# Experts of a decoder block on one core: w1 and w3 held by TensorE, tokens passed through

## The chip, the cores and the metric

The kernel runs on 1 core of one Trainium2 chip. The metric is the device time of the whole kernel in microseconds. TensorE's clock has two levels here, 1.2 and 2.4 GHz; the profile gives the granted clock of a stretch as a share of the higher one.

## The reference, cut to what matters

A decoder block with layer norm behind each part runs on x of 32 sequences x 128 tokens x 128 features, f32: first a state space layer, then cross attention, then a mixture of 8 experts. Each token goes to its best two experts, and an expert is

```
h   = silu(x @ w1[e].T) * (x @ w3[e].T)        # 128 -> 512, twice
out = out + wte[:, e] * (h @ w2[e].T)          # 512 -> 128
```

The product with w2 sums over the 512 values of h. A TensorE product sums over partitions, so both of its operands must have h's 512 values on partitions (in 4 chunks of 128).

## The kernel before, in words

**Stages.** The state space layer and the attention take the first 840 us: 8 groups of 4 sequences, in an order written out by hand for each engine. Every token's row is scattered to two places in DRAM (`xg`), one area per expert. Then a table is built on VectorE: for each of NT = 72 tiles of 128 rows, its expert and its first row. The expert stage goes over the 72 tiles, and the last stage adds the two results of each token and normalises.

**The expert stage.** Each engine has its own loop over tiles, and semaphores order them. In the words of the code, with b the parity of the tile:

- SyncE, `rows_in` (L387 to L389): reads the tile's first row from the table and starts the load of 128 rows to `xs` (named qk in the profile), 4 buffers.
- TensorE, `rows_t` (L1677): transposes the rows to bank 7. `up` (L1679 to L1683): `value_load` reads the expert from the table (L1680), then two products of 512 columns, with the tokens `xsT` as the held operand and w1 or w3 passing, to bank b (named pair_a; w1) and bank 2+b (pair_b; w3). `gated_t` (L1688): 4 transposes of the gated rows, to bank 4+b (y_ps). `down` (L1691 to L1696): another `value_load`, then 4 products with w2 (named prob), summed in bank 6.
- ScalarE: `x_out` (L829) copies the transposed rows to `xsT` (qk), `silu` (L833) turns bank b into `sl` (zabs), and the copy at L846 brings the transposed gated rows to `gT` (decays).
- VectorE: `gate` (L1191) multiplies `sl` by bank 2+b into `gg` (zpos). The copy at L1232 empties bank 6 into `ys` (aoT). `destinations` (L1196 to L1200) are three operations on 128x1 for a later tile's scatter. In the first 8 tiles `gate_gaps` adds up to one operation a tile.
- GpSimd (L566) scatters `ys` to `y2` in DRAM, 4 buffers.

**The order.** In turn j, TensorE issues rows_t(j+3), up(j+2), gated_t(j+1), down(j). VectorE issues gate(j+2), the copy of y(j), destinations(j+3). down(j) waits at L1694 and L1695: for gT of tile j, and until j copies at L1232 are done (`y_sb` starts at 1), that is those of tiles 0 to j-1. gate(j) waits until both products of up(j) are done (`up_ps`) and for silu(j). After the loop SyncE waits for the last scatters, and loads the results with `results_in` (L407); three of the four buffers of these loads are parts of `u` and `sres`.

Of the kernel before, what the change touches and what calls it, by code (L numbers as in the profile page):

```python
# [9 lines left out]
ACT = mybir.ActivationFunctionType  # L10
AX = mybir.AxisListType

P = 128
# [6 lines left out]
E, F = 8, 512  # L20
FC = F // P
STRIDE = B * L + P
NT = (2 * B * L + E * (P - 1)) // P + 1
# [21 lines left out]
def build(nc, a, out):  # L45
    ctx = ExitStack()
    with ctx:
        def sb(name, shape, dt=F32):
            return ctx.enter_context(nc.sbuf_tensor(name, shape, dt))

        def sem(name):
            return ctx.enter_context(nc.semaphore(name))

        ident = sb("ident", [P, P])
# [36 lines left out]
        w1 = sb("w1", [P, E, F])  # L91
        w3 = sb("w3", [P, E, F])
# [12 lines left out]
        u = sb("u", [P, 2, 2, T])  # L105
# [8 lines left out]
        decays = sb("decays", [P, 2, 2 * T])  # L114
# [27 lines left out]
        w2 = prob[:, :, :, :, :].rearrange("p a j c m -> p (a j) c m")  # L142
# [45 lines left out]
        table = sb("table", [P, 2, NT + 8], I32)  # L188
# [3 lines left out]
        xsT = free[:, 4 * ROW:4 * ROW + 2 * P].rearrange("p (b n) -> p b n", b=2)  # L192
        sl = zabs
        gg = zpos
        gT = decays[:, 0, :].rearrange("p (b c n) -> p b c n", b=2, c=FC)
        ys = aoT[:, 0:4 * D].rearrange("p (b d) -> p b d", b=4)
        spare = sb("spare", [P, 8])
        place = sb("place", [P, 8])
# [12 lines left out]
        bank = [x[:, i] for x in (pair_a, pair_b, y_ps) for i in range(2)]  # L211
# [13 lines left out]
        pad_sb mask_sb s_ps s_neg p_sb rden_sb rden_wide_sb pT_ps pT_sb pTd_sb pv_ps rdenT_ps rdenT_sb rdenTd_sb aoT_sb wo_ps  # L225
        ln2_stat ln2_var ln2_log ln2_rstd x2_sb x2T_ps x2T_sb lg_ps lg_sb route rank_ps pos_sb row_sb scat
        tail tail_store table_sb table_link gap_sb gexp_sb gate_link
        xs_load0 xs_load1 xs_load2 xs_load3 xsT_ps xsT_sb up_ps silu_sb gate_sb gT_ps gT_sb y_ps_s y_sb place_sb dest_sb y_out0 y_out1 y_out2 y_out3
        yk_load0 yk_load1 yk_load2 yk_load3 yk_sb acc_ps f_stat f_var f_log f_rstd fin_sb fin_store0 fin_store1""".split()
        s = {n: sem(n) for n in names}  # L230

# [66 lines left out]
        def parts(m):  # L298

            return (m - 1 if m else None), (m + 1 if m + 1 < G else None), (m + 2 if m + 2 < G else None)  # L300
# [5 lines left out]
        def _(sp):  # L306
# [90 lines left out]
            with sp.Fori(0, NT // 4) as it:  # L397
                for b in range(4):
                    j = it * 4 + b
# [6 lines left out]
            def results_in(g, b):  # L406
                sp.dma_start(yk[b].rearrange("p (s k) d -> p s (k d)", k=2), y2r[g]).then_inc(s[f"yk_load{b}"], 16)  # L407
# [4 lines left out]

            for b in range(4):
                sp.wait_ge(s[f"y_out{b}"], NT // 4 * 16)
            for b in range(4):
                results_in(b, b)
            for g in range(G):
# [153 lines left out]
        def _(act):  # L571
            A = nc.scalar.activation
# [175 lines left out]
            for m in range(G):  # L748
                w, e, c = parts(m)
# [77 lines left out]
            def x_out(j, b):  # L827
                act.wait_ge(s["xsT_ps"], 1 + j + 1)
                A(xsT[:, b, :], bank[7][:, b * P:(b + 1) * P], ACT.Copy).then_inc(s["xsT_sb"], 1)  # L829

            def silu(j, b):
                act.wait_ge(s["up_ps"], 1 + 2 * j + 1)
                A(sl[:, b, :], bank[b], ACT.Silu).then_inc(s["silu_sb"], 1)  # L833

            nc.scalar.preload_act_table_set("silu_and_others")
            x_out(0, 0)
            x_out(1, 1)
            silu(0, 0)
            act.wait_ge(s["up_ps"], 1 + 2)
            x_out(2, 0)  # L840
            silu(1, 1)
            with act.Fori(0, NT // 2) as it:
                for b in range(2):
                    j = it * 2 + b
                    act.wait_ge(s["gT_ps"], j + 1)
                    A(gT[:, b], bank[4 + b].rearrange("p (c n) -> p c n", c=FC), ACT.Copy).then_inc(s["gT_sb"], 1)  # L846
                    x_out(j + 3, 1 - b)
                    silu(j + 2, b)
            nc.scalar.preload_act_table_set("natural_log_exp_and_others")
            act.wait_ge(s["gap_sb"], 1)  # L850
            A(gexp, gap, ACT.Exp, scale=-1.0).then_inc(s["gexp_sb"], 1)
# [25 lines left out]
        def _(dve):  # L877
            v_ = nc.vector
# [12 lines left out]
            for h in range(2):  # L891
                last = v_.tensor_scalar(d_diag[:, h, :], ident[:, :], d_col[:, h:h + 1], None, ALU.mult)
# [182 lines left out]
            for m in range(G):  # L1075
                w, e, c = parts(m)
# [111 lines left out]
            def gate(j, b):  # L1188
                dve.wait_ge(s["up_ps"], 1 + 2 * j + 2)
                dve.wait_ge(s["silu_sb"], j + 1)  # L1190
                TT(gg[:, b, :], sl[:, b, :], bank[2 + b], ALU.mult).then_inc(s["gate_sb"], 1)  # L1191

            def destinations(j, load, turn, slot):
                dve.wait_ge(s[f"xs_load{load}"], turn * 16 + 16)
                second = xs[:, load, D + 1:D + 2]
                v_.tensor_scalar(spare[:, slot:slot + 1], second, 0.0, j128[:, bass.ds(j, 1)], ALU.is_lt, ALU.mult)  # L1196
                v_.scalar_tensor_tensor(place[:, slot:slot + 1], second, t_e[:, bass.ds(j, 1)], xs[:, load, D:D + 1],
                                        ALU.is_equal, ALU.add).then_inc(s["place_sb"], 1)
                dve.wait_ge(s["place_sb"], j + 1)
                TT(dest[:, slot:slot + 1], spare[:, slot:slot + 1], place[:, slot:slot + 1], ALU.add).then_inc(s["dest_sb"], 1)  # L1200
# [24 lines left out]
            def eight_tiles(it):  # L1225
                for b in range(8):
                    j = it * 8 + b
                    gate(j + 2, b % 2)
                    dve.wait_ge(s["y_ps_s"], j + 1)
                    if not (isinstance(it, int) and b < 4):  # L1230
                        dve.wait_ge(s[f"y_out{b % 4}"], (2 * it + b // 4) * 16)
                    v_.tensor_copy(ys[:, b % 4, :], bank[6][:, b % 2 * P:(b % 2 + 1) * P]).then_inc(s["y_sb"], 1)  # L1232
                    destinations(j + 3, (b + 3) % 4, 2 * it + (b + 3) // 4, (b + 3) % 8)
                    if isinstance(it, int):
                        gate_gaps(b)

            for j in range(3):
                destinations(j, j, 0, j)
            gate(0, 0)
            gate(1, 1)  # L1240
            eight_tiles(0)
            with dve.Fori(1, NT // 8) as it:
                eight_tiles(it)
# [36 lines left out]
        def _(pe):  # L1280
            MM = nc.tensor.matmul
            TR = nc.tensor.transpose
# [301 lines left out]
            for m in range(G):  # L1584
                w, e, c = parts(m)
# [88 lines left out]
            def rows_t(j, b, turn, load):  # L1674
                pe.wait_ge(s[f"xs_load{load}"], turn * 16 + 16)
                pe.wait_ge(s["xsT_sb"], j)
                TR(bank[7][:, b * P:(b + 1) * P], xs[:, load, 0:D], ident[:, :]).then_inc(s["xsT_ps"], 1)  # L1677

            def up(j, b):  # L1679
                e = pe.value_load(table[0:1, 0, bass.ds(j, 1)], min_val=0, max_val=E - 1)  # L1680
                pe.wait_ge(s["xsT_sb"], j + 1)
                MM(bank[b], xsT[:, b, :], w1[:, bass.ds(e, 1), :].rearrange("p a f -> p (a f)"), start=True, stop=True).then_inc(s["up_ps"], 1)  # L1682
                MM(bank[2 + b], xsT[:, b, :], w3[:, bass.ds(e, 1), :].rearrange("p a f -> p (a f)"), start=True, stop=True).then_inc(s["up_ps"], 1)  # L1683

            def gated_t(j, b):
                pe.wait_ge(s["gate_sb"], 1 + j + 1)
                for c in range(FC):
                    last = TR(bank[4 + b][:, c * P:(c + 1) * P], gg[:, b, c * P:(c + 1) * P], ident[:, :])  # L1688
                last.then_inc(s["gT_ps"], 1)

            def down(j, b):  # L1691
                e = pe.value_load(table[0:1, 0, bass.ds(j, 1)], min_val=0, max_val=E - 1)
                pe.wait_ge(s["gT_sb"], j + 1)
                pe.wait_ge(s["y_sb"], 1 + j)  # L1694
                for c in range(FC):  # L1695
                    last = MM(bank[6][:, b * P:(b + 1) * P], gT[:, b, c, :], w2[:, bass.ds(e, 1), c, :].rearrange("p a d -> p (a d)"),  # L1696
                              start=(c == 0), stop=(c == FC - 1))
                last.then_inc(s["y_ps_s"], 1)

            pe.wait_ge(s["table_sb"], 1)  # L1700
            pe.wait_ge(s["w13_load"], 32)
            pe.wait_ge(s["w2_load"], 16)
            rows_t(0, 0, 0, 0)
            rows_t(1, 1, 0, 1)
            up(0, 0)
            rows_t(2, 0, 0, 2)
            up(1, 1)
            gated_t(0, 0)
            with pe.Fori(0, NT // 4) as it:
                for b in range(4):  # L1710
                    j = it * 4 + b
                    rows_t(j + 3, 1 - b % 2, it + (b + 3) // 4, (b + 3) % 4)
                    up(j + 2, b % 2)
                    gated_t(j + 1, 1 - b % 2)
                    down(j, b % 2)

            def sums(g):
                at(pe, "fin_sb", S * (g - 3))
# [51 lines left out]
```

## Time and profile before

| | |
|---|---|
| median of 3 runs | 1138.08 us (1131.46 to 1140.45) |
| profiled execution | 1135.38 us |
| its span | 1133.5 us, granted clock 0.951 on average |
| TensorE busy | 962.6 us, 85% of the span |
| VectorE busy | 697.1 us, 62% |
| ScalarE busy | 720.5 us, 64% |
| GpSimd busy | 576.0 us, 51% |

The span runs from the first to the last instruction, and 1.9 us lie around it. Busy shares are means over stages that have different limits. The expert stage runs from about 857 to 1093 us.

### The profile page before, as it was taken

The page shows a single profiled execution, that of the slowest core. Times are in us where ns is not written, and L with a number is a line of the kernel's source. Part 1 is how long each engine was busy: PE and PEld are TensorE (multiplying, and loading weights), DVE is VectorE, ACT ScalarE, POOL GpSimd, SP SyncE. Part 2 cuts the span into 40 slices and gives each one's busy share as a digit, 9 for nine tenths or more (in the row PEclk, how much of TensorE's full clock was granted, in tenths as well). Part 3 has the DMA queues.
Part 4 walks back from the last instruction along what each step waited for, and adds up shares of the span by engine and source line. Part 5 has one row for each costly group of instructions (what it writes and reads, how often), then busy time and mean ns, then how long its engine had stood idle before and what let it go on. Part 6 is the DMA issues. An engine that isn't in the chain of part 4 may idle for free.

```text
span 1133.5 us, 28078 instructions
## 1 busy us (share of the span) xinstructions
PE 962.6 (85%) x9703; PEld 543.2 (48%) x9704; DVE 697.1 (62%) x1371; ACT 720.5 (64%) x2212; POOL 576.0 (51%) x395
## 2 busy tenths in 40 slices
PE   6799889989788888979888885976937999999997
PEld 2344544444354445435444542543434666666662
DVE  0467667786577767657766794796653544444437
ACT  3567966876696677669667882964822444444446
POOL 2578258457726954782696388268041333333320
PEclk9889999999899999989999996998977999999999
DMA  4606104201500520050042005003131111111134
GB/s 113 138 15 132 30 1 96 66 2 38 133 12 4 124 54 3 17 136 28 4 107 60 4 16 137 2 4 118 50 119 44 41 41 42 42 42 42 42 105 151
DMA packets 69227, 66.69 MB, mean 59 GB/s; under 512 B 9728, under 2 KB 63104, under 8 KB 68736
## 3 DMA queue, kind: packets, MB, share of 16 engines
q1 hardware_dynamic: 63856, 55.59, 19.8%
q0 software_dynamic: 4352, 8.99, 2.4%
q8 instruction: 69, 1.13, 0.4%
q10 hardware_dynamic: 912, 0.67, 0.2%
q14 instruction: 38, 0.31, 0.1%
HBM read 49.09 MB, written 16.13 MB: 58 GB/s over the span
## 4 chain that ended last, share of the span: by engine, by line
PE 45%; POOL 21%; issue 20%; ACT 8%; DVE 5%; DMA 1%; SPq 0%; POOLq 0%; DVEq 0%; ACTq 0%
POOL hst L494 8%; PE pair_a L1682 6%; PE pair_b L1683 6%; PE bank L1696 6%; POOL prob L494 6%; ACT prob L692 5%; POOL xg L526 4%; PE y_ps L1404 3%; PE y_ps L1688 3%; PE pair_b L1484 3%; PE bank L1302 2%; PE y_ps L1484 2%; PE bank L1495 2%; PE pair_a L1518 2%; PE pair_a L1382 1%
## 5 line engine op out<-in xcount | busy, mean ns | idle before, releaser
L651 ACT ACTIVATE decays<-w,a_neg 128x256 f32<-128x256 f32 x512 | 220.5, 509 | 30.2 <-DVE hst L920 17.6
L494 POOL TENSOR_TENSOR hst<-hst,c_rep 128x1024 f32<-128x1024 f32 x64 | 151.4, 2372 | 73.8 <-DVE hst L920 73.1
L494 POOL TENSOR_TENSOR prob<-prob,c_rep 128x1024 f32<-128x1024 f32 x56 | 133.2, 2381 | 57.3 <-DVE prob L920 56.7
L566 POOL DMA_INDIRECT y<-aoT,dest x72 | 69.6, 966 | 173.2 <-DVE aoT L1232 168.8
L920 DVE TENSOR_TENSOR_SCAN prob<-decays,pair_b 128x1024 f32<-128x1024 f32 x32 | 73.1, 2284 | 69.4 <-issue 54.6
L692 ACT ACTIVATE prob<-pair_b,nmax 128x128 f32<-128x128 f32 x256 | 90.4, 399 | 22.4 <-DVE nmax L974 22.3
L1191 DVE TENSOR_TENSOR zpos<-zabs,pair_b 128x512 f32<-128x512 f32 x74 | 50.8, 687 | 81.3 <-PE pair_b L1683 80.2
L1404 PE MATMUL y_ps<-hst,sum 128*32 128x256 f32 x512 | 74.4, 442 | 24.4 <-POOL prob L494 24.4
L692 ACT ACTIVATE prob<-y_ps,nmax 128x128 f32<-128x128 f32 x256 | 90.8, 415 | 0.0
L526 POOL DMA_INDIRECT xg<-x_all,pos x64 | 64.8, 1013 | 35.8 <-DVE pos L1066 23.7
L920 DVE TENSOR_TENSOR_SCAN prob<-decays,pair_a 128x1024 f32<-128x1024 f32 x32 | 73.0, 2281 | 13.5 <-ACT decays L651 9.9
L1682 PE MATMUL pair_a<-w,qk 128*128 x148 | 77.7, 607 | 0.5 <-ACT qk L829 0.5
L1683 PE MATMUL pair_b<-w,qk 128*128 x148 | 76.5, 599 | 0.0
L1696 PE MATMUL bank<-prob,decays 128*128 x576 | 76.1, 275 | 0.0
L1495 PE MATMUL bank<-ident,prob 128*128 128x128 f32 x512 | 70.7, 279 | 5.3 <-ACT pT L702 5.3
L846 ACT ACTIVATE decays<-y_ps 128x512 f32<-128x512 f32 x72 | 43.0, 598 | 50.2 <-PE y_ps L1688 49.5
L1404 PE MATMUL y_ps<-prob,sum 128*32 128x256 f32 x512 | 74.5, 442 | 0.0
L1382 PE MATMUL pair_b<-w,du_tok 64*32 64x256 f32 x2048 | 72.1, 390 | 2.4 <-DVE prob L920 2.3
L486 POOL TENSOR_TENSOR w<-diag,b_tok 128x1024 f32<-128x1024 f32 x32 | 60.6, 1925 | 26.3 <-ACT b_tok L633 26.3
L920 DVE TENSOR_TENSOR_SCAN hst<-decays,pair_b 128x1024 f32<-128x1024 f32 x32 | 72.6, 2270 | 1.6 <-PE pair_b L1382 1.6
L833 ACT ACTIVATE zabs<-pair_a 128x512 f32<-128x512 f32 x74 | 44.2, 597 | 45.4 <-PE pair_a L1682 45.4
L1302 PE MATMUL bank<-xT,w_conv 128*128 128x512 f32 x112 | 62.1, 676 | 10.1 <-ACT xT L581 10.1
(281 smaller groups left out, 2186.0 us busy)
## 6 DMA issues: line engine op xcount, KB each, us to landing
w<-d_dram SPq DMA_DIRECT2D x64, 256.0 KB
c_rep<-c_dram SPq DMA_DIRECT2D x64, 128.0 KB, 3.4
qk<-xg SPq DMA_DIRECT2D x79, 65.0 KB, 1.9
d_dram<-zpos SPq DMA_DIRECT2D x8, 512.0 KB, 3.0
xn<-in_x SPq DMA_DIRECT2D x8, 256.0 KB, 3.0
cn<-in_ctx SPq DMA_DIRECT2D x8, 256.0 KB, 3.3
mask_b<-in_mask SPq DMA_DIRECT2D x8, 256.0 KB, 3.4
w<-in_w1T SPq DMA_DIRECT2D x1, 2048.0 KB, 8.4
```

The lines of the kernel that those rows point to most:

```text
L494: g_.tensor_tensor(by_state(ring(k)), by_state(ring(k)), c_rep[:, :, toks[r]].rearrange("p q (i t) -> p i q t", i=2), ALU.mult).then_inc(s ...
L526: pool.indirect_dma_start(xg[:, :], bass.IndirectOffsetOnAxis(ap=pos[:, t, k:k + 1], axis=0), x2_all[:, w * S + t, :], None).then_inc(s["s ...
L651: last = A(by_state(decays[:, k % 2, :])[:, :, q, :], delta_rep[:, b, toks[r]].rearrange("p (i t) -> p i t", i=2), ACT.Exp, scale=a_neg[:, ...
L692: last = A(prob[:, t % 2, c, j, :], bank[2 + c][:, j * L:(j + 1) * L], ACT.Exp, bias=nmax[:, t % 2, h:h + 1], accum_out=den[:, t % 2, h:h ...
L920: v_.tensor_tensor_scan(ring(k), decays[:, k % 2, :], pair(k)[:, :, :].rearrange("p i c -> p (i c)"), 0.0, ALU.mult, ALU.add).then_inc(s[" ...
L1302: last = MM(bank[b].rearrange("p (s t) -> p s t", s=S), w_conv[:, k, h * P:(h + 1) * P], xT[:, :, k:k + L], start=(k == 0), stop=(k == KCO ...
L1382: last = MM(pair(k)[32 * j:32 * j + 32, i, :].rearrange("p (q y t) -> p q y t", q=NQ, y=2)[:, :, y, :], du_tok[half, r, y, 32 * b:32 * b + ...
L1404: last = MM(y_ps[32 * i:32 * i + 32, r, h * HT:(h + 1) * HT].rearrange("p (i t) -> p i t", i=2), sum32[:, :], by_state(ring(4 * x + i))[:, ...
L1495: last = TR(bank[6 + c % 2][:, j * L:(j + 1) * L], prob[:, t % 2, c, j, :], ident[:, :])
L1682: MM(bank[b], xsT[:, b, :], w1[:, bass.ds(e, 1), :].rearrange("p a f -> p (a f)"), start=True, stop=True).then_inc(s["up_ps"], 1)
L1683: MM(bank[2 + b], xsT[:, b, :], w3[:, bass.ds(e, 1), :].rearrange("p a f -> p (a f)"), start=True, stop=True).then_inc(s["up_ps"], 1)
L1696: last = MM(bank[6][:, b * P:(b + 1) * P], gT[:, b, c, :], w2[:, bass.ds(e, 1), c, :].rearrange("p a d -> p (a d)"), start=(c == 0), stop= ...
```

## The change

The tokens now pass and the weights are held. In `up`, 4 chunks of w1 and then 4 of w3 are the held operands, with `xsT` passing, 128 columns each, so that the products come out with the 512 values on partitions. `gated_t`, its copy at L846 and `gT` are gone, and `down` takes `gg` itself. The held operands come from `w13`, two buffers in the storage of `u`: ScalarE copies the expert's w1 there (`hold_w1`), VectorE its w3 (`hold_w3`), each with a `value_load` of its own for the expert, 4 tiles ahead; TensorE's `value_load` in `up` is gone.

The orders change too. TensorE: rows_t(j+3), down(j), up(j+2). VectorE: gate(j+2), hold_w3(j+4), the copy of y(j), destinations(j+3). ScalarE: x_out(j+3), silu(j+2), a wait for both products of up(j+2), hold_w1(j+4). SyncE gets three more waits ahead of the loads of results.

```diff
             def up(j, b):
-                e = pe.value_load(table[0:1, 0, bass.ds(j, 1)], min_val=0, max_val=E - 1)
                 pe.wait_ge(s["xsT_sb"], j + 1)
-                MM(bank[b], xsT[:, b, :], w1[:, bass.ds(e, 1), :].rearrange("p a f -> p (a f)"), start=True, stop=True).then_inc(s["up_ps"], 1)
-                MM(bank[2 + b], xsT[:, b, :], w3[:, bass.ds(e, 1), :].rearrange("p a f -> p (a f)"), start=True, stop=True).then_inc(s["up_ps"], 1)
-
-            def gated_t(j, b):
-                pe.wait_ge(s["gate_sb"], 1 + j + 1)
+                pe.wait_ge(s["w1_sb"], j + 1)
                 for c in range(FC):
-                    last = TR(bank[4 + b][:, c * P:(c + 1) * P], gg[:, b, c * P:(c + 1) * P], ident[:, :])
-                last.then_inc(s["gT_ps"], 1)
+                    last = MM(bank[b][:, c * P:(c + 1) * P], w13[:, b, 0, c * P:(c + 1) * P], xsT[:, b, :], start=True, stop=True)
+                last.then_inc(s["up_ps"], 1)
+                pe.wait_ge(s["w3_sb"], j + 1)
+                for c in range(FC):
+                    last = MM(bank[2 + b][:, c * P:(c + 1) * P], w13[:, b, 1, c * P:(c + 1) * P], xsT[:, b, :], start=True, stop=True)
+                last.then_inc(s["up_ps"], 1)
 
             def down(j, b):
...
-                pe.wait_ge(s["gT_sb"], j + 1)
+                pe.wait_ge(s["gate_sb"], 1 + j + 1)
                 pe.wait_ge(s["y_sb"], 1 + j)
...
                     rows_t(j + 3, 1 - b % 2, it + (b + 3) // 4, (b + 3) % 4)
+                    down(j, b % 2)
                     up(j + 2, b % 2)
-                    gated_t(j + 1, 1 - b % 2)
-                    down(j, b % 2)
```

On VectorE, ScalarE and SyncE:

```diff
+            def hold_w3(j, b):
+                e = dve.value_load(table[0:1, 0, bass.ds(j, 1)], min_val=0, max_val=E - 1)
+                v_.tensor_copy(w13[:, b, 1, :], w3[:, bass.ds(e, 1), :].rearrange("p a f -> p (a f)")).then_inc(s["w3_sb"], 1)
...
                     gate(j + 2, b % 2)
+                    hold_w3(j + 4, b % 2)
                     dve.wait_ge(s["y_ps_s"], j + 1)
...
+            def hold_w1(j, b):
+                e = act.value_load(table[0:1, 0, bass.ds(j, 1)], min_val=0, max_val=E - 1)
+                A(w13[:, b, 0, :], w1[:, bass.ds(e, 1), :].rearrange("p a f -> p (a f)"), ACT.Copy).then_inc(s["w1_sb"], 1)
...
-                    act.wait_ge(s["gT_ps"], j + 1)
-                    A(gT[:, b], bank[4 + b].rearrange("p (c n) -> p c n", c=FC), ACT.Copy).then_inc(s["gT_sb"], 1)
                     x_out(j + 3, 1 - b)
                     silu(j + 2, b)
+                    act.wait_ge(s["up_ps"], 1 + 2 * j + 6)
+                    hold_w1(j + 4, b)
...
+            sp.wait_ge(s["up_ps"], 1 + 2 * (NT + 2))
+            sp.wait_ge(s["w1_sb"], NT + 4)
+            sp.wait_ge(s["w3_sb"], NT + 4)
```

Ahead of the loops, the first four tiles' weights are copied between the first `x_out`, `silu`, `destinations` and `gate` calls.

## Rows read from the trace of the kernel before

**Rows 1.** Busy time by engine (instructions), clock, DMA share, GB/s: the tiles' stretch.

```profile
869.06:1093.37 224.31, 224.31 (x1209) 152.88 (x1209) 101.67 (x361) 105.53 (x214) 68.55 (x71) 1.00 0.15 42
```

**Rows 2.** One line's instructions: ns min/median/max, first and last start us.

```profile
L1232 DVE COPY aoT<-bank x72: 291/291/292, 869.1 to 1093.4; 128x128 f32<-128x128 f32 x72
```

**Rows 3.** Timeline, one tile: start us, us, engine line op [idle before].

```profile
951.15 1.02 PE L1682 MATMUL pair_a<-w,qk 128*128 x2
...
952.01 1.02 PE L1683 MATMUL pair_b<-w,qk 128*128 x2
...
952.87 0.60 PE L1688 MATMUL y_ps<-ident,zpos 128*128 128x128 f32 x4
...
953.07 0.69 DVE L1191 TENSOR_TENSOR zpos<-zabs,pair_b 128x512 f32<-128x512 f32 x1 [1.10 <-PE pair_b L1683]
953.20 0.97 PEld L1696 LDWEIGHTS bank<-prob,decays 128*128 128x128 f32 x8
953.31 1.06 PE L1696 MATMUL bank<-prob,decays 128*128 x8
...
954.20 0.27 PE L1677 MATMUL bank<-ident,qk 128*128 128x128 f32 x1
...
954.31 1.02 PE L1682 MATMUL pair_a<-w,qk 128*128 x2
954.40 0.29 DVE L1232 COPY aoT<-bank 128x128 f32<-128x128 f32 x1 [0.64 <-PE bank L1696]
...
954.61 0.20 DVE L1196 TENSOR_SCALAR spare<-qk,j 128x1 f32<-128x1 f32 x1
```

**Rows 4.** Groups by line, 900 to 1060 us: busy us, mean ns, idle before.

```profile
L1682 PE MATMUL pair_a<-w,qk 128*128 x102 | 52.2, 594 | 0.0
...
L1696 PEld LDWEIGHTS bank<-prob,decays 128*128 128x128 f32 x405 | 49.2, 192 | 0.0
```

**Rows 5.** By line, 952.8 to 954 us (L1231: to 956.3): a value load, VectorE's sequencer.

```profile
L1680 PEldq FUSED_REGOPS  x2: 46/98/151, 952.8 to 953.3; - x2
L1680 PEldq TENSOR_LOAD <-table x1: 302/302/302, 952.9 to 952.9; - x1
...
L1682 PEldq FUSED_REGOPS  x1: 46/46/46, 953.6 to 953.6; - x1
...
L1231 DVEq EVENT_SEMAPHORE  x2: 21/21/21, 953.1 to 956.2; - x2
```

**Rows 6.** VectorE's groups over the whole span, shapes apart.

```profile
L989 DVE COPY pT<-bank 128x512 f32<-128x512 f32 x32 | 21.4, 670 | 0.0
...
L1216 DVE TENSOR_SCALAR decays<-decays 128x512 f32<-128x512 f32 x1 | 0.4, 421 | 0.0
```

**Rows 7.** Timeline, a weight load that waits for VectorE, in the attention.

```profile
709.81 0.72 DVE L962 TENSOR_SCALAR x<-pair_a,mv,rstd 128x128 f32<-128x128 f32 x2
...
710.58 0.14 PEld L1458 LDWEIGHTS pair_a<-ident,x 128*128 128x128 f32 x1 [0.30 <-DVE x L962]
```

**Rows 8.** Timeline, the end of the stage.

```profile
1093.09 0.63 ACT L851 ACTIVATE hst<-decays 128x512 f32<-128x512 f32 x1
...
1093.37 0.29 DVE L1232 COPY aoT<-bank 128x128 f32<-128x128 f32 x1 [0.64 <-PE bank L1696]
...
1096.11 0.55 DVE L1253 RECIPROCAL gates_all<-hst 128x64 f32<-128x64 f32 x1
...
1097.16 0.38 SPq L407 DMA_DIRECT2D c_rep<-y  x1
...
1101.38 2.44 ACT L860 ACTIVATE c_rep<-c_rep,gates_all 128x128 f32<-128x128 f32 x8 [7.66 <-DMA c_rep<-y]
```

**Rows 9.** Busy time by engine and clock in stretches with a partly idle TensorE.

```profile
744.50:749.00 4.50, 2.25 (x47) 1.20 (x39) 4.46 (x8) 2.10 (x6) 2.38 (x1) 1.00 0.00 0
749.00:753.50 4.50, 2.80 (x72) 1.44 (x74) 4.50 (x7) 3.33 (x8) 3.41 (x2) 1.00 0.02 4
...
834.50:839.00 4.50, 2.41 (x11) 1.92 (x9) 1.07 (x13) 1.94 (x3) 3.52 (x4) 0.50 0.55 216
```

More of the change, by code:

```diff
@@ L194, in build @@
         gg = zpos
-        gT = decays[:, 0, :].rearrange("p (b c n) -> p b c n", b=2, c=FC)
+        w13 = u
         ys = aoT[:, 0:4 * D].rearrange("p (b d) -> p b d", b=4)
@@ L227, in build @@
         tail tail_store table_sb table_link gap_sb gexp_sb gate_link
-        xs_load0 xs_load1 xs_load2 xs_load3 xsT_ps xsT_sb up_ps silu_sb gate_sb gT_ps gT_sb y_ps_s y_sb place_sb dest_sb y_out0 y_out1 y_out2 y_out3
+        xs_load0 xs_load1 xs_load2 xs_load3 xsT_ps xsT_sb up_ps w1_sb w3_sb silu_sb gate_sb y_ps_s y_sb place_sb dest_sb y_out0 y_out1 y_out2 y_out3
         yk_load0 yk_load1 yk_load2 yk_load3 yk_sb acc_ps f_stat f_var f_log f_rstd fin_sb fin_store0 fin_store1""".split()
@@ L833, in silu @@
                 A(sl[:, b, :], bank[b], ACT.Silu).then_inc(s["silu_sb"], 1)
+            def hold_w1(j, b):
+                e = act.value_load(table[0:1, 0, bass.ds(j, 1)], min_val=0, max_val=E - 1)
+                A(w13[:, b, 0, :], w1[:, bass.ds(e, 1), :].rearrange("p a f -> p (a f)"), ACT.Copy).then_inc(s["w1_sb"], 1)
             nc.scalar.preload_act_table_set("silu_and_others")
+            act.wait_ge(s["table_sb"], 1)
+            act.wait_ge(s["w13_load"], 32)
+            hold_w1(0, 0)
+            hold_w1(1, 1)
             x_out(0, 0)
@@ L840, in _ @@
             x_out(2, 0)
+            hold_w1(2, 0)
             silu(1, 1)
+            act.wait_ge(s["up_ps"], 1 + 4)
+            hold_w1(3, 1)
             with act.Fori(0, NT // 2) as it:
@@ L1235, in eight_tiles @@
                         gate_gaps(b)
+            dve.wait_ge(s["table_sb"], 1)
+            dve.wait_ge(s["w13_load"], 32)
+            hold_w3(0, 0)
+            hold_w3(1, 1)
             for j in range(3):
@@ L1239, in _ @@
             gate(0, 0)
+            hold_w3(2, 0)
             gate(1, 1)
+            hold_w3(3, 1)
             eight_tiles(0)
@@ L1679, in up @@
             def up(j, b):
-                e = pe.value_load(table[0:1, 0, bass.ds(j, 1)], min_val=0, max_val=E - 1)
                 pe.wait_ge(s["xsT_sb"], j + 1)
-                MM(bank[b], xsT[:, b, :], w1[:, bass.ds(e, 1), :].rearrange("p a f -> p (a f)"), start=True, stop=True).then_inc(s["up_ps"], 1)
-                MM(bank[2 + b], xsT[:, b, :], w3[:, bass.ds(e, 1), :].rearrange("p a f -> p (a f)"), start=True, stop=True).then_inc(s["up_ps"], 1)
-            def gated_t(j, b):
-                pe.wait_ge(s["gate_sb"], 1 + j + 1)
+                pe.wait_ge(s["w1_sb"], j + 1)
                 for c in range(FC):
-                    last = TR(bank[4 + b][:, c * P:(c + 1) * P], gg[:, b, c * P:(c + 1) * P], ident[:, :])
-                last.then_inc(s["gT_ps"], 1)
+                    last = MM(bank[b][:, c * P:(c + 1) * P], w13[:, b, 0, c * P:(c + 1) * P], xsT[:, b, :], start=True, stop=True)
[4 more added lines that the diff above has]
+                last.then_inc(s["up_ps"], 1)
             def down(j, b):
                 e = pe.value_load(table[0:1, 0, bass.ds(j, 1)], min_val=0, max_val=E - 1)
-                pe.wait_ge(s["gT_sb"], j + 1)
+                pe.wait_ge(s["gate_sb"], 1 + j + 1)
                 pe.wait_ge(s["y_sb"], 1 + j)
                 for c in range(FC):
-                    last = MM(bank[6][:, b * P:(b + 1) * P], gT[:, b, c, :], w2[:, bass.ds(e, 1), c, :].rearrange("p a d -> p (a d)"),
+                    last = MM(bank[6][:, b * P:(b + 1) * P], gg[:, b, c * P:(c + 1) * P], w2[:, bass.ds(e, 1), c, :].rearrange("p a d -> p (a d)"),
                               start=(c == 0), stop=(c == FC - 1))
@@ L1700, in _ @@
             pe.wait_ge(s["table_sb"], 1)
-            pe.wait_ge(s["w13_load"], 32)
             pe.wait_ge(s["w2_load"], 16)
@@ L1707, in _ @@
             up(1, 1)
-            gated_t(0, 0)
             with pe.Fori(0, NT // 4) as it:
```

## The prediction

> **What bounds the kernel now.** I read the busy shares by stage first. In the stretch from the first tile's copy to the last's, TensorE is busy all 224.31 us at a granted clock of 1.00, the 2.4 GHz level, while VectorE is busy 102 us, ScalarE 106 and GpSimd 69 [rows 1]. Between the first and the last start of the copy at L1232 lie 71 steps [rows 1, 2]: 224.31 / 71 = 3.159 us a tile. The timeline of one tile [rows 3] shows what fills it, from start to start on TensorE: w1 0.86 us (951.15 to 952.01), w3 0.86, the four transposes 0.44 (952.87 to 953.31), down 0.89 (953.31 to 954.20), the rows' transpose 0.11. That is 3.16, with no gap, and TensorE idles before none of its groups [rows 4]. So TensorE's columns are the bound, and the other engines' waits cost nothing.
>
> What the reader should see in the order of the code is why that holds. down(j) waits for the copy of y(j-1), which stands on VectorE behind gate(j+1), and gate(j+1) waits for up(j+1). Before, TensorE has gated_t(j), down(j-1), rows_t(j+3), up(j+2) and gated_t(j+1) to do between the end of up(j+1) and down(j), 0.44 + 0.89 + 0.11 + 1.72 + 0.44 = 3.6 us, and VectorE is done well within it.
>
> **The change part by part.**
>
> *TensorE's columns.* Removed: four transposes, 0.44 us a tile. The two products of 512 columns become 16 passes of 128 columns with 16 weight loads: down is already 8 such loads and 8 such passes in 0.89 us, 0.111 each [rows 3], so up takes 16 x 0.111 = 1.78 where it took 1.72, 0.06 more. TensorE's work is 0.11 + 0.89 + 1.78 = 2.78 us a tile, 0.38 less than now. Were it still the bound, the kernel would lose 72 x 0.38 = 27 us. One rule of the Trainium skill speaks against this: "TensorE: Matmul & The Clock Gate", part 3, under what overlaps, has a weight load overlap running products only where it goes to other row groups; all these loads fill all rows. By it each load would stand between two passes. The trace differs: the 8 loads of down start at 953.20 and take 0.97 us beside passes that start at 953.31 and make way for the next line after 0.89 [rows 3]. I take 0.111 each.
>
> *The new order, and the wait that it makes.* Now down(j) comes before up(j+2), so directly behind up(j+1), with only rows_t(j+3), 0.11 us, between. Its wait at L1695 has not changed: it asks for the copy of y(j-1). On VectorE that copy stands behind gate(j+1) and now also behind hold_w3(j+3), and gate(j+1) waits for the last column of up(j+1). So in every turn TensorE ends up(j+1) and stands until VectorE has done three operations. Counted from T, the end of up's columns:
>
> 1. last column to gate: 0.20 us (952.87 to 953.07, rows 3).
> 2. gate: 0.69. An operation that needs nothing of the one ahead starts some 0.08 before that one's end (954.40 + 0.29 = 954.69 against 954.61, rows 3), so the next could start 0.61 after gate did. But hold_w3 begins with a value load, whose register work no row shows for VectorE. On TensorE it runs from 952.8 to 953.6 [rows 5], 0.8 us, of which reading the table is 0.302. VectorE's sequencer runs ahead of its engine: it takes up the wait at L1231 at 953.1, when gate has just started [rows 3, 5]. So I let the 0.8 run from gate's start, beside gate: the copy starts at T + 1.00 rather than T + 0.81. Lower end: wholly hidden, 0.19 less. Upper end: it begins when gate is done, T + 0.89 + 0.8 = 1.69, 0.69 more. The row at L1231 is nearest, hence the middle.
> 3. hold_w3's copy, 128x512 f32 from SBUF to SBUF: not in the trace. Nearest is L1216, one such input and output in SBUF, 0.421 us; a copy of that size out of PSUM takes 0.670 [rows 6]. I take 0.42, less 0.08 of overlap, 0.34; upper end 0.25 more.
> 4. the copy of y: 0.29, ends at T + 1.63.
> 5. to TensorE: a weight load started at 710.58 when VectorE was done at 709.81 + 0.72 = 710.53 [rows 7]: 0.05 at least; I take 0.10, since two operations are merged in that row. From load to first pass 0.11 (953.20 to 953.31, rows 3). down starts at T + 1.84.
>
> Then down 0.89 and up 1.78 end at T + 4.51. That is the new period: 4.51 - 3.16 = 1.35 us more a tile, over 71 steps 96 us. TensorE's rows_t lies inside the stall.
>
> *ScalarE.* It loses the copy at L846 and gains hold_w1. Behind both products of up: 0.20, value load 0.8 with nothing beside it, copy 0.63 (the ACTIVATE of 128x512 in SBUF at L851, rows 8): T + 1.6, then x_out at T + 1.9. That xsT is needed by the next turn's rows_t at T + 4.5, and this w1 by an up nearly two turns on. silu waits for w1's half of up, which ends 0.89 before T, and takes 0.60: done at 0.1 before T, ahead of gate's start. All of it costs nothing, with 2.6 us of slack; the cover is the stall itself. In a turn of 2.78 us it would still have 0.9.
>
> *TensorE's value load* in down stands ahead of its waits, inside the stall: 0.8 under 1.84. The one in up goes, hidden before too.
>
> *SyncE and GpSimd.* rows_in has the same waits, with more time; the new waits after the loop are for up, hold_w1 and hold_w3 of the last tiles, over at T + 1.7, when the scatter behind the copy of y, which ended at 1093.66, let the first load of results go at 1097.16 [rows 8], 3.5 us later: at T + 5.1 now. Nothing. The gates' chain on VectorE (done by 1096.7, results first used at 1101.38, rows 8) gains some 2 us ahead of it and keeps as much. `gate_gaps` comes after the copy of y, so in the first tiles it delays the next gate only if it runs over 2.8 us: no.
>
> *The ends.* The first copy of y now stands behind gate(2) and hold_w3(4), with a saved transpose: about 1 us later. The last is again the end of the same chain.
>
> **Sum.** 1135.4 + 96 + 1 = 1232 us against the profiled execution's own time. That execution lies 0.24% under the median of the three runs, so the figure for a median is some 1 to 3 us higher: 1233.
>
> **The rivals.**
>
> *A, faster: the wait has room and TensorE's columns stay the bound.* 1135 - 27 = 1108 us. It decides from the point where the way from up's end to down's start is under 0.38 + 0.11 = 0.49 us. For it: TensorE's work does fall to 2.78, and every other engine has less than that. Against: gate's own 0.69 and its 0.20 of way are in the chain, whatever the rest takes. Only if I misread the order could it win: 4%.
>
> *B, slower still: VectorE's value load waits until gate is done*, or hold_w3 reads slowly. The first adds 0.69 a tile, 49 us: 1281. The second adds 0.25, 18 us: 1250. For it: no register load stands on VectorE in this trace. Against: L1231 in rows 5. The first 12%, the second 8%.
>
> *C, the clock falls.* TensorE is now busy 2.78 of 4.51 us, 62%, with 1.7 us idle in each. Against: in stretches that are busy 50% and 62% the granted clock is 1.00, the 2.4 GHz level [rows 9]. For: at 54%, between attention and experts, it is 0.50, the 1.2 GHz level, so the share alone does not settle it. If it did fall to 1.2 GHz, down and up would take 5.34 instead of 2.67: 71 x 2.67 = 190 us more, 1423. 4%.
>
> *D, the weight loads stand in line.* By rows 3 one step of load and pass is 0.111; a load in line would add as much again, 24 times a tile, but down's 8 are in the row and do not. With 16 more at 0.111, 1.78 x 71 = 126 more, 1359. The rule named above is this one. 1%.
>
> **How the numbers follow.** The forecast, with the load beside gate, has 70%, and 1% is left for a stall that just cancels the gain. Its own bounds: with the value load hidden (0.19), and the way to TensorE at 0.05, 4.27 a tile, 1215. On the high side rows of the attention, where engines collide, have the same shapes some hundredths longer; 1245. The likeliest time is 1233. The range takes in B: 1211 to 1283, leaving out A, C and D and what lies beyond the bounds, some 12%. A measurement of this kernel can tell about 1% from no change. Faster by over 1%: A, 0.04. Within 1%: only if the stall came to just 0.49 us, 0.01. Slower: 0.95.
>
> **What would show it.** In the profile after: starts of the copy at L1232's successor 4.5 us apart; TensorE idle about 1.7 us before the first pass of down, put down to VectorE's copy; the 16 passes of up 0.111 apart; on VectorE gate, hold_w3's copy and the copy of y one behind the other, starting 0.2 us after up; the clock at 1.00; ScalarE waiting before x_out and silu. The step to doubt first is the start of hold_w3's copy: 0.8 us after gate's start if the sequencer runs ahead, 1.5 if not. The prediction is wrong if down does not wait for VectorE at all, or if the tiles are under 3.1 us apart.

## The result and the profile after

The changed kernel takes 1243.09 us (median of 4, 1241.6 to 1245.74) against 1137.64 us for the kernel before in the same comparison: a ratio of 1.0938, interval 1.0889 to 1.0987. It is 9.4% slower. 1233 was forecast, with 1211 to 1283 as its range. The profiled execution took 1245.74 us, the longest of the four, with a span of 1243.8. Medians and ratios here count executions in the fast state alone; two in the slow one are left out, 3645.63 us in the last experiment and 2364.71 us of the kernel before beside it.

The first fence is the busy time of the stretch from the start of the first copy of y to 1201.00, shortly after that of the last but one, in the columns of rows 1; the second has all of that copy's instructions, now L1252, in those of rows 2.

```profile
869.61:1201.00 331.39, 216.56 (x1763) 200.15 (x1764) 124.02 (x431) 97.86 (x212) 68.37 (x71) 0.99 0.10 28
```

```profile
L1252 DVE COPY aoT<-bank x72: 283/284/286, 869.6 to 1203.6; 128x128 f32<-128x128 f32 x72
```

71 steps now take 1203.64 - 869.61 = 334.0 us, 4.705 us a tile where it was 3.159 [rows 1, 2]. That is 1.546 x 71 = 109.8 us more, and the two profiled executions are 110.4 apart. The rest is level: the first copy starts 0.55 us later, and from the last copy's start to the end of the span it is 40.2 us in both. TensorE, busy all the time before, is busy 65% of the stretch.

The mean clock of 0.99 hides one drop. In the ninth turn, TensorE stood 2.13 us before down's passes, where it is 1.64 in the turn shown below. Then, from some point behind 908 us, the clock was 0.50, the 1.2 GHz level, until about 911.8, and 1.00 from there to the last copy:

```profile
907.23 1.15 PE L1722 MATMUL bank<-prob,zpos 128*128 x8 [2.13 <-DVE aoT L1252]
...
909.75 1.91 PE L1714 MATMUL pair_b<-qk,u 128*128 128x128 f32 x8
911.46 0.42 PE L1703 MATMUL bank<-ident,qk 128*128 128x128 f32 x1
```

```profile
909.00:911.00 2.00, 2.00 (x11) 2.00 (x11) 0.00 (x0) 0.60 (x1) 0.00 (x0) 0.50 0.25 66
912.00:1203.64 291.64, 190.15 (x1562) 176.01 (x1563) 107.47 (x374) 86.77 (x187) 59.37 (x62) 1.00 0.10 28
```

up took 3.24 us there (908.22 to 911.46) instead of 1.79, so the drop cost some 1.5 us once. The longer wait ahead of it came from VectorE: the copy of w3 started 1.22 us behind gate's start instead of 0.84, in the first turn that VectorE does inside its loop (its first eight turns are written out ahead of it). Why, no row shows. The copies of y tell the same: the first seven steps take 4.57 us each (869.61 to 901.62), the eighth 5.08 (to 906.70), the ninth 6.20 (to 912.90), and the other 62 take 4.69 each.

One tile in the timeline (start us, us, engine, line, idle before; what answers to rows 3). T, the end of up's columns, is 1005.24, where the next transpose starts.

```profile
1004.35 1.06 PE L1714 MATMUL pair_b<-qk,u 128*128 128x128 f32 x8
...
1005.24 0.27 PE L1703 MATMUL bank<-ident,qk 128*128 128x128 f32 x1
1005.44 0.69 DVE L1206 TENSOR_TENSOR zpos<-zabs,pair_b 128x512 f32<-128x512 f32 x1 [2.78 <-PE pair_b L1714]
1006.14 0.63 ACT L841 ACTIVATE u<-w 128x512 f32 x1 [0.99 <-PE pair_b L1714]
1006.28 0.43 DVE L1210 COPY u<-w 128x512 f32 x1
1006.62 0.28 DVE L1252 COPY aoT<-bank 128x128 f32<-128x128 f32 x1
1006.68 0.26 ACT L833 ACTIVATE qk<-bank 128x128 f32<-128x128 f32 x1
...
1007.15 0.97 PEld L1722 LDWEIGHTS bank<-prob,zpos 128*128 128x128 f32 x8 [1.87 <-issue]
1007.15 1.15 PE L1722 MATMUL bank<-prob,zpos 128*128 x8 [1.64 <-DVE aoT L1252]
...
1008.03 0.97 PEld L1710 LDWEIGHTS pair_a<-qk,u 128*128 128x128 f32 x8
1008.14 1.06 PE L1710 MATMUL pair_a<-qk,u 128*128 128x128 f32 x8
...
1009.04 1.06 PE L1714 MATMUL pair_b<-qk,u 128*128 128x128 f32 x8
...
1009.93 0.27 PE L1703 MATMUL bank<-ident,qk 128*128 128x128 f32 x1
```

Read it as a ring. up ends at 1005.24. VectorE, which had idled 2.78 us for it, does gate, hold_w3's copy and the copy of y one behind the other. Only then does down start on TensorE, at 1007.15, and up follows it: 1009.93 - 1005.24 = 4.69 us. From 1007.15 on it is 2.78 us, as forecast: 0.11 from down's first load to its first pass, and 2.67 for down and up. The other 1.91 are the way through VectorE, with the rows' transpose inside them. The chain of waits through the same tile tells it by engine, with the sequencers' steps (start us, us, what):

```profile
1005.44 0.07 DVE zpos L1206
...
1005.55 0.31 DVEq L1209
1005.85 0.04 issue
1005.89 0.19 DVEq L1209
...
1006.18 0.06 DVEq L1210
...
1006.28 0.06 DVE u L1210
...
1006.62 0.30 DVE aoT L1252
1006.92 0.24 issue
1007.15 1.15 PE bank L1722 x8
```

L1209 is the value load. It runs beside gate, which is busy until 1006.13. The copy behind it starts 0.15 us after that; an operation with nothing between starts some 0.08 before the end of the one ahead (1006.62 against 1006.28 + 0.43), so the value load costs 0.23.

### The profile page after: what moved, and what is told of

Same layout as the page of the kernel before. It is cut to its first block, busy times and chain, and to the rows that moved or that the text cites. A ratio compares the mean times of both kernels' runs of the same rounds, so it can differ in the third digit from the quotient of the medians.

```text
span 1243.8 us, 29739 instructions
## 1 busy us (share of the span) xinstructions
PE 954.8 (77%) x10299; PEld 594.9 (48%) x10300; DVE 719.9 (58%) x1448; ACT 716.3 (58%) x2217; POOL 576.1 (46%) x395
## 4 chain that ended last, share of the span: by engine, by line
PE 42%; issue 20%; POOL 16%; DVE 8%; ACT 8%; DVEq 4%; DMA 1%; SPq 1%; another core or an unknown queue 0%; POOLq 0%; ACTq 0%
PE bank L1722 7%; POOL hst L498 6%; PE pair_b L1714 5%; PE pair_a L1710 5%; ACT prob L696 5%; POOL prob L498 4%; PE y_ps L1430 3%; DVEq L1209 3%; POOL xg L530 3%; PE pair_b L1510 2%; PE bank L1328 2%; PE y_ps L1510 2%; PE bank L1521 2%; DVE aoT L1252 2%; PE pair_a L1408 2%
## 5 line engine op out<-in xcount | busy, mean ns | idle before, releaser
L1722 PE MATMUL bank<-prob,zpos 128*128 x576 | 82.9, 287 | 115.8 <-DVE aoT L1252 115.8
L1722 PEld LDWEIGHTS bank<-prob,zpos 128*128 128x128 f32 x576 | 69.7, 191 | 132.5 <-issue 132.5
L841 ACT ACTIVATE u<-w 128x512 f32 x76 | 47.9, 630 | 85.1 <-PE pair_b L1714 72.4
L1710 PE MATMUL pair_a<-qk,u 128*128 128x128 f32 x592 | 80.0, 279 | 0.0
L935 DVE TENSOR_TENSOR_SCAN prob<-decays,pair_a 128x1024 f32<-128x1024 f32 x32 | 72.9, 2280 | 12.1 <-ACT decays L655 10.8
L1714 PE MATMUL pair_b<-qk,u 128*128 128x128 f32 x592 | 79.9, 279 | 0.0
L1710 PEld LDWEIGHTS pair_a<-qk,u 128*128 128x128 f32 x592 | 73.8, 196 | 0.0
L1714 PEld LDWEIGHTS pair_b<-qk,u 128*128 128x128 f32 x592 | 73.8, 196 | 0.0
```

The source lines that it names most:

```text
L935: v_.tensor_tensor_scan(ring(k), decays[:, k % 2, :], pair(k)[:, :, :].rearrange("p i c -> p (i c)"), 0.0, ALU.mult, ALU.add).then_inc(s[" ...
L1710: last = MM(bank[b][:, c * P:(c + 1) * P], w13[:, b, 0, c * P:(c + 1) * P], xsT[:, b, :], start=True, stop=True)
L1714: last = MM(bank[2 + b][:, c * P:(c + 1) * P], w13[:, b, 1, c * P:(c + 1) * P], xsT[:, b, :], start=True, stop=True)
L1722: last = MM(bank[6][:, b * P:(b + 1) * P], gg[:, b, c * P:(c + 1) * P], w2[:, bass.ds(e, 1), c, :].rearrange("p a d -> p (a d)"), start=(c ...
```

## The experiments

**Down in two banks, asking for the copy before last.** Beside the lines below, the counts that GpSimd and the last stage wait for are one higher, and the idle products ahead of the last stage go to bank 6.

```diff
-            early(dve, "gate_sb y_sb")
+            early(dve, "gate_sb y_sb y_sb")
...
-                    v_.tensor_copy(ys[:, b % 4, :], bank[6][:, b % 2 * P:(b % 2 + 1) * P]).then_inc(s["y_sb"], 1)
+                    v_.tensor_copy(ys[:, b % 4, :], bank[4 + b % 2][:, 0:P]).then_inc(s["y_sb"], 1)
...
-                    last = MM(bank[6][:, b * P:(b + 1) * P], gg[:, b, c * P:(c + 1) * P], w2[:, bass.ds(e, 1), c, :].rearrange("p a d -> p (a d)"),
+                    last = MM(bank[4 + b][:, 0:P], gg[:, b, c * P:(c + 1) * P], w2[:, bass.ds(e, 1), c, :].rearrange("p a d -> p (a d)"),
```

> The changed kernel with down's sum in two banks instead of the two halves of bank 6 (the banks that the transposes have left), and down(j) asking for the copy of y(j-2) instead of that of y(j-1). Every engine's work and order stay. Theory (the loss is TensorE's wait for the copy of y behind gate and hold_w3): the wait of 1.9 us a tile is gone, TensorE's columns bind at 2.78 us a tile, and the kernel takes 1135 - 27 = 1108 to 1115 us, under the kernel before. Rival (the held weights cost the time: loads that do not overlap, register work on TensorE, or the copies w1 and w3): stays at 1235 to 1245 us.

Measured: 1108.33 us, ratio to the kernel before 0.9771 (0.9747 to 0.9796). The theory holds, and the rival, that the held weights cost the time, falls: they are all still held here, and copied by the same engines. Busy time by engine in this kernel from 900 to 1040 us, and the start of one turn in its timeline:

```profile
900.00:1040.00 140.00, 139.93 (x1254) 139.69 (x1254) 86.08 (x300) 69.66 (x151) 48.13 (x51) 1.00 0.17 47
```

```profile
1000.56 0.27 PE L1703 MATMUL bank<-ident,qk 128*128 128x128 f32 x1
...
1000.67 1.06 PE L1722 MATMUL y_ps<-prob,zpos 128*128 x8
...
1000.85 0.69 DVE L1206 TENSOR_TENSOR zpos<-zabs,pair_b 128x512 f32<-128x512 f32 x1 [0.98 <-PE pair_b L1714]
```

down starts 0.11 us behind the transpose, ahead even of gate; TensorE has no gap. Its weight loads are busy 139.7 of 140 us beside products that are busy 139.9: each of the 25 loads of a tile lies beside a pass.

**VectorE's copy of y first.**

```diff
             def eight_tiles(it):
...
-                    gate(j + 2, b % 2)
-                    hold_w3(j + 4, b % 2)
                     dve.wait_ge(s["y_ps_s"], j + 1)
...
+                    gate(j + 2, b % 2)
+                    hold_w3(j + 4, b % 2)
                     destinations(j + 3, (b + 3) % 4, 2 * it + (b + 3) // 4, (b + 3) % 8)
```

> The changed kernel with VectorE's order alone altered: the copy of y(j) first, then gate(j+2) and hold_w3(j+4). Theory: down(j+1) no longer stands behind gate(j+2), so TensorE's columns bind, 1108 to 1118 us. Margin by the rows: the copy of y(j+1) is ready 1.0 + 0.2 us into a turn, but VectorE is at hold_w3 and the destinations until some 2 us after up's end, so it ends about 2.4 us into a turn of 2.78 and down(j+2) comes later still. Rival (any work of VectorE between up and down delays it): 1180 to 1245 us.

Measured: 1106.89 us, ratio 0.9757 (0.9733 to 0.9781). No bank and no wait is altered here, only the order of three operations in VectorE's queue, and the time falls by 136 us. The two kernels can't be told apart, since TensorE's columns bind in both. The margin is small: in most turns the copy of y ends 2.1 us behind T, in some 2.6, in a turn of 2.79. One of the late ones, with T before it at 1000.20:

```profile
1002.53 0.29 DVE L1250 COPY aoT<-bank 128x128 f32<-128x128 f32 x1 [0.43 <-issue]
...
1002.99 0.27 PE L1703 MATMUL bank<-ident,qk 128*128 128x128 f32 x1
1003.07 0.97 PEld L1722 LDWEIGHTS bank<-prob,zpos 128*128 128x128 f32 x8
1003.10 1.13 PE L1722 MATMUL bank<-prob,zpos 128*128 x8
```

The copy ends at 1002.82 and down's weight load, which could have gone at 1002.99, goes at 1003.07, 0.25 behind the copy's end.

**hold_w3 behind the copy of y.**

```diff
                     gate(j + 2, b % 2)
-                    hold_w3(j + 4, b % 2)
...
+                    hold_w3(j + 4, b % 2)
                     destinations(j + 3, (b + 3) % 4, 2 * it + (b + 3) // 4, (b + 3) % 8)
```

> The changed kernel with hold_w3 behind the copy of y: gate(j+2), copy of y(j), hold_w3(j+4). Theory: the copy of y starts 0.61 us after gate instead of 1.18 (1006.62 - 1005.44), so each turn is 0.57 us shorter: 71 x 0.57 = 40 us less, about 1203 us. Rival (the value load holds up VectorE's queue wherever it stands): within 10 us of the changed kernel.

Measured: 1199.77 us, ratio 1.0584 (1.0557 to 1.0611), 43 us under the changed kernel, as forecast but for 3 us. Its timeline, with T = 1002.61:

```profile
1002.61 0.27 PE L1703 MATMUL bank<-ident,qk 128*128 128x128 f32 x1
1002.80 0.69 DVE L1206 TENSOR_TENSOR zpos<-zabs,pair_b 128x512 f32<-128x512 f32 x1 [2.24 <-PE pair_b L1714]
1003.41 0.28 DVE L1251 COPY aoT<-bank 128x128 f32<-128x128 f32 x1
...
1003.73 0.43 DVE L1210 COPY u<-w 128x512 f32 x1
1003.94 0.97 PEld L1722 LDWEIGHTS bank<-prob,zpos 128*128 128x128 f32 x8 [1.30 <-issue]
```

The copy of y starts 0.61 behind gate's start and down 1.33 behind T, where it was 1.91. That is 0.58 less, beside 0.57 by which the copy of y starts sooner. So what stands between gate and that copy is paid for in full in each turn, and hold_w3 behind it costs nothing here.

**The order alone, on the kernel before.**

```diff
                     rows_t(j + 3, 1 - b % 2, it + (b + 3) // 4, (b + 3) % 4)
+                    down(j, b % 2)
                     up(j + 2, b % 2)
                     gated_t(j + 1, 1 - b % 2)
-                    down(j, b % 2)
```

> The kernel before, tokens held and transposes kept, with TensorE's order of the change: rows_t(j+3), down(j), up(j+2), gated_t(j+1). Theory (the order makes the loss): down(j+1) now waits for VectorE's copy behind gate(j+2), 0.2 + 0.61 + 0.29 + 0.25 = 1.35 us after up's end, and for ScalarE's copy of the transposed rows, 0.44 + 0.2 + 0.6 + 0.2 = 1.45 us after it, where 0.55 us of its own work lies between: about 1.0 us more a tile, 71 us, 1205 to 1215 us. Rival (the held weights make it): 1130 to 1145 us, as before.

Measured: 1229.02 us, ratio 1.0841 (1.0812 to 1.0871). So with tokens held and transposes kept, the order by itself makes a loss of the same kind. The size was missed: 1.31 us a tile, not 1.0. The timeline shows both parts:

```profile
1000.43 0.60 PE L1688 MATMUL y_ps<-ident,zpos 128*128 128x128 f32 x4
...
1001.07 0.60 ACT L846 ACTIVATE decays<-y_ps 128x512 f32<-128x512 f32 x1 [0.70 <-PE y_ps L1688]
1001.24 0.28 DVE L1232 COPY aoT<-bank 128x128 f32<-128x128 f32 x1
...
1001.80 0.97 PEld L1696 LDWEIGHTS bank<-prob,decays 128*128 128x128 f32 x8 [0.90 <-issue]
...
1003.07 0.30 PEld L1682 LDWEIGHTS pair_a<-w,qk 128*128 128x128 f32 x2 [0.30 <-issue]
```

down's first load waits until 1001.80, mostly for ScalarE's copy, as expected; with nothing to wait for it would go with the rows' transpose at 1000.87, so that is 0.93 us. But then up comes 1.27 us later, where down needs 0.89: up's value load stands on TensorE's sequencer behind down's wait, starts at 1002.3 and is over by 1003.0. 0.93 + 0.38 is the 1.31. A value load that cost nothing while the sequencer ran ahead is laid bare by a wait in front of it. The changed kernel has no value load in up, and is spared this.

**No value load on VectorE.**

```diff
-                e = dve.value_load(table[0:1, 0, bass.ds(j, 1)], min_val=0, max_val=E - 1)
-                v_.tensor_copy(w13[:, b, 1, :], w3[:, bass.ds(e, 1), :].rearrange("p a f -> p (a f)")).then_inc(s["w3_sb"], 1)
+                v_.tensor_copy(w13[:, b, 1, :], w3[:, 0, :]).then_inc(s["w3_sb"], 1)
```

> The changed kernel with hold_w3 copying expert 0's w3 always, so that VectorE has no value load (the output's experts are wrong in w3; sizes and number of copies stay). Theory (the value load runs beside gate and sticks out by what the trace shows, 0.84 between gate's start and the copy's against 0.61 for operations back to back): 0.2 us less a tile, and with the address work gone about 16 us in all, 1224 to 1232 us. Rival (the value load's whole 0.8 us is in the chain): 57 us less, 1186 us.

Measured: 1227.04 us, ratio 1.083 (1.0797 to 1.0862), 16 us under the changed kernel. Gate starts at 1001.22 in its timeline and the copy of w3 at 1001.83:

```profile
1001.22 0.69 DVE L1206 TENSOR_TENSOR zpos<-zabs,pair_b 128x512 f32<-128x512 f32 x1 [2.79 <-PE pair_b L1713]
1001.83 0.42 DVE L1209 COPY u<-w 128x512 f32<-128x512 f32 x1
```

0.61 against 0.84: the value load costs 0.23 us a turn, times 71 about the 16 measured. Rival B of the prediction, a load that waits until gate is done, falls: had it waited, taking it out would have gained 0.8 us a turn, 57 us. So does B's other half, a slow read of w3: the copy takes 0.43 us, not the 0.67 of a copy out of PSUM.

**No address to work out for w2.**

```diff
-                e = pe.value_load(table[0:1, 0, bass.ds(j, 1)], min_val=0, max_val=E - 1)
                 pe.wait_ge(s["gate_sb"], 1 + j + 1)
...
-                    last = MM(bank[6][:, b * P:(b + 1) * P], gg[:, b, c * P:(c + 1) * P], w2[:, bass.ds(e, 1), c, :].rearrange("p a d -> p (a d)"),
+                    last = MM(bank[6][:, b * P:(b + 1) * P], gg[:, b, c * P:(c + 1) * P], w2[:, 0, c, :],
```

> The changed kernel with down always on expert 0's w2 and without its value load (the output's experts are wrong in w2). Theory (of the 0.25 us between the end of the copy of y and down's first weight load, the forecast had 0.10; the other 0.15 is TensorE's sequencer that works out w2's address behind the wait): 0.1 to 0.15 us less a tile, 7 to 11 us, 1231 to 1236 us. Rival (0.25 is the way of a semaphore from VectorE's copy out of PSUM): no change, 1243 us.

Measured: 1233.69 us, ratio 1.0881 (1.0843 to 1.092). That interval overlaps the changed kernel's, 1.0889 to 1.0987, so the times alone say little; the trace decides it. The copy of y ends at 1001.75 + 0.28 = 1002.03 and down's first weight load starts 0.11 us later, not 0.25. The 71 steps between the copies of y take 1193.9 - 869.6 = 324.3 us, 9.7 less than in the changed kernel, of which its one drop of the clock is 1.5:

```profile
1001.75 0.28 DVE L1252 COPY aoT<-bank 128x128 f32<-128x128 f32 x1
...
1002.14 0.97 PEld L1721 LDWEIGHTS bank<-prob,zpos 128*128 128x128 f32 x8 [1.74 <-DVE zpos L1206]
```

In the changed kernel, TensorE's sequencer takes up the wait for the copy of y (L1720) at 1006.9 and has the register operations of L1722 from 1007.1 on:

```profile
L1720 PEldq EVENT_SEMAPHORE  x1: 51/51/51, 1006.9 to 1006.9; - x1
...
L1722 PEldq FUSED_REGOPS  x4: 46/46/46, 1007.1 to 1007.4; - x4
```

This experiment takes out the value load of down too, but that one was covered: it stands ahead of the wait, and the one for the next tile runs at 1008.1 to 1008.7, 3 us before it is needed. What is left as the cause is the address of the first product, worked out from the loaded register only once the wait is over. Its register operation is 0.046 us of the 0.14; what fills the rest, no row shows.

## Why the prediction was right, step by step

The mechanism is the one that was forecast. TensorE stands because down(j) asks for a copy which stands on VectorE behind gate(j+1), and this gate for the product just ended. Taking away the wait (two banks) or the order in front of it (copy first) turns 1243 us into 1108 and 1107. Putting TensorE's new order alone into the kernel before gives 1229, there with ScalarE's copy as the last to be waited for.

*TensorE's columns.* Forecast: 2.78 us a tile, 0.111 for each load with its pass, and 1108 us were they the bound. Right: the changed kernel did not go the way of rival A, but the two-bank kernel did, at 1108.33. One figure of rival A was off: at a way of 0.49 us the stall only cancels the gain. For TensorE's columns to bind, the way would have to be under 0.11, the rows' transpose. The rule of the Trainium skill ("TensorE: Matmul & The Clock Gate", part 3), that a weight load overlaps only where the row groups differ, does not hold for these loads: eight loads of 128x128 and their passes take 0.89 us in every group of the turn shown, and the two-bank kernel's loads are busy 139.69 of 140 us beside its passes.

*The ring, term by term*, forecast against the tile shown, counted from T: gate starts at 0.20 against 0.20; hold_w3's copy at 1.00 against 1.04; the copy of y ends at 1.63 against 1.66; down's first load at 1.73 against 1.91. The term that was too small is step 5, the way from VectorE to TensorE: 0.10 forecast, 0.25 measured. The row that it was taken from shows a weight load with a fixed address. Behind down's wait the address of w2 has to be worked out first, 0.14 us of the 0.25 by the last experiment. With the 0.03 of VectorE this is the 0.18 by which the tile shown misses the forecast period, 4.69 against 4.51: 11 us over the 62 turns like it. The nine turns ahead of them add 3 more, over half of it by the clock's drop. For the profiled execution 1232 was forecast, and it took 1245.74, 14 more. The medians are only 10 apart, 1243.09 against 1233, since the changed kernel's profiled execution is 2.65 us above its median, and the one before was under its own.

*The value load* was rightly laid beside gate, and rightly not wholly hidden: 0.84 us from gate's start to the copy's, 0.8 forecast. The size of the copy, 0.43 us, is that of the row chosen for it.

*The clock* was 1.00 with TensorE busy 65%, but for the one drop that cost 1.5 us. Rival C, a clock that falls and stays down, did not come, but the forecast had no term for a single drop. Whether the 2.13 us wait ahead of it was the cause is not shown: without w2's address TensorE waited 2.03 us in the same turn, and the clock stayed at 1.00. *ScalarE* ended x_out 1.70 us behind T, 1.9 forecast, and nobody waited for it. *The ends*: the first copy was forecast 1 us later from the stage's start. It came 11.0 us behind the first transpose instead of 12.1, so 1 us sooner. Most of it is up's value load on TensorE, which had nothing to hide behind at the start: from the second transpose to up's first load it was 0.98 us (857.92 to 858.90) and is 0.07 (859.58 to 859.65). On the trace's clock the first copy starts 0.55 us later all the same, since the first transpose comes at 858.62 instead of 857.01. That is no effect of the change that any run shows: in the eight kernels profiled it comes anywhere from 853.77 to 859.36.

Nothing here tells how TensorE would fare if it could take the held weights straight from w1 and w3: that was not tried.

## What to carry to other kernels

When a step is moved ahead in one engine's queue, read its waits again, although none has changed, and follow each back to what the same engine now issues directly in front of it: if the two meet, the pipeline has become a ring, and every operation between them on the other engine is paid for in each turn. The cure is cheap compared with the loss: here, the order of three operations in VectorE's queue turned 9.4% slower into 2.4% faster, and a second bank for down's sum into 2.3%, with the same work on every engine. Inside such a ring, look also for register loads that stand behind a wait (0.38 us a turn in one experiment) and for a computed address in the first instruction behind it (0.14 us). Moving the one or the other elsewhere was not tried; here they were only taken out, or put in.

## What the runs showed of the hardware

- A value load on VectorE takes some 0.7 us from its first register step to the last (1005.5 to 1006.24), on TensorE 0.8 [rows 5]. VectorE's sequencer does it beside the operation in flight: it is 0.84 us from the start of a 0.69 us operation to that of the copy that uses the value, 0.61 without the load. In the first eight tiles, where the tile's number is a constant and not a loop's register, it is 873.85 - 873.12 = 0.73.
- Working out a product's address behind a wait added 0.14 us ahead of TensorE's first weight load (0.25 against 0.11 from the end of VectorE's copy).
- A value load behind a wait on TensorE's sequencer left a gap of 1.27 - 0.89 = 0.38 us, where the same load ahead of time had left none.
- Full 128x128 f32 weight loads lie beside running passes: 25 loads a tile, busy 139.69 of 140 us, beside passes that are busy 139.93.
- TensorE, busy 65% with a gap of 1.64 us in each turn of 4.69, was granted the full clock for 291 us on end. The one drop to 0.50 came after a gap of 2.13 us; after one of 2.03 us in another kernel none came.
